# A gated attention stage on one Trainium2 core: the decay's products moved behind the weighted sums, and two ScalarE steps reordered

## What is computed

```python
# q = layernorm(x); k = v = ctx; 4 heads of 64; 64 sequences of 128 tokens
ig = concat(q, k, v) @ igate + b_i;  fg = concat(q, k, v) @ fgate + b_f
cs = cumsum(log_sigmoid(fg))
log_D = where(lower_triangle, cs - cs.T, -inf) + ig.T
m = max(log_D, axis=-1)
D = exp(log_D - m)
C = (qh @ kh.T) / sqrt(64) * D
normalizer = maximum(abs(sum(C, axis=-1)), exp(-m))
h = (C / (normalizer + 1e-6)) @ vh
x = x + tanh(g) * (layernorm_per_head(h) * outnorm_scale)
```

## Time and profile before

| | us |
|---|---|
| three runs | 1446.23, 1447.42, 1459.62 |
| median | 1447.42 |
| span of the profiled execution, first to last instruction | 1446.3 |

### The profile page before, as it was taken

The page is one execution under the profiler, slowest core; times in us unless marked ns, Lnnn a source line. Parts: engine busy times, 40 slices in busy tenths (PEclk is TensorE's granted clock), DMA queues, the critical chain, the costliest instruction groups (busy, mean ns, idle before and its releaser), DMA issues.

```text
span 1446.3 us, 30872 instructions
## 1 busy us (share of the span) xinstructions
PE 1327.5 (92%) x11617; PEld 896.8 (62%) x11672; DVE 1163.6 (80%) x1888; ACT 1050.8 (73%) x1739; POOL 769.1 (53%) x1225
## 2 busy tenths in 40 slices
PE   4799999999999999999997999999889988579898
PEld 3466666666666666666654666666667666434376
DVE  3577887887888878877786999998656899979988
ACT  2377777777777777777764988888745665689897
POOL 2156666767668667675767333441302586878100
PEclk9999999999999999999987999999999998889999
DMA  9666867758668576676530000000255463229099
GB/s 151 112 127 110 132 114 132 133 97 150 107 122 136 99 144 112 108 124 105 90 98 1 1 1 1 1 1 1 70 157 149 105 163 96 51 122 401 1 379 377
DMA packets 124964, 165.71 MB, mean 115 GB/s; under 512 B 47362, under 2 KB 78210, under 8 KB 120450
## 3 DMA queue, kind: packets, MB, share of 16 engines
q1 hardware_dynamic: 124048, 162.95, 49.8%
q10 hardware_dynamic: 768, 0.79, 0.5%
HBM read 76.07 MB, written 35.65 MB: 77 GB/s over the span
## 4 chain that ended last, share of the span: by engine, by line
PE 64%; DVE 13%; ACT 11%; issue 4%; POOL 4%; DMA 2%; SPq 1%; ACTq 0%; DVEq 0%; POOLq 0%
PE psum L574 10%; PE psum L585 10%; PE psum L561 7%; PE psum L602 5%; PE psum L549 4%; PE psum L619 4%; PE psum L982 4%; PE psum L1013 3%; ACT f_gelu L2071 3%; PE psum L1005 3%; ACT f_gelu L2063 2%; PE psum L523 2%; PE psum L536 2%; POOL a_fac L1772 2%; PE psum L612 2%
## 5 line engine op out<-in xcount | busy, mean ns | idle before, releaser
L764 DVE TENSOR_REDUCE neg_max<-psum 128x8 f32<-128x1024 f32 x256 | 313.1, 1223 | 67.9 <-PE psum L561 63.2
L695 ACT ACTIVATE exp_t<-psum 128x512 f32<-128x512 f32 x512 | 281.5, 597 | 49.6 <-PE psum L574 49.5
L869 POOL TENSOR_TENSOR rs<-rs,minus_half 128x16 f32<-128x16 f32 x64 | 186.4, 2912 | 5.0
L574 PEld LDWEIGHTS psum<-q_stack,k_stack 50*128 50x128 f32 x2048 | 135.0, 188 | 77.5 <-issue 73.2
L574 PE MATMUL psum<-q_stack,k_stack 50*128 50x128 f32 x2048 | 171.1, 287 | 0.8 <-ACT exp_t L695 0.8
L585 PE MATMUL psum<-exp_t,v_pad 128*32 128x256 f32 x2048 | 165.8, 396 | 0.0
L561 PE MATMUL psum<-k_stack,q_stack 48*128 48x256 f32 x1024 | 133.4, 339 | 14.9 <-DVE neg_max L764 11.3
L700 ACT ACTIVATE o_t<-psum 128x512 f32<-128x512 f32 x128 | 76.7, 599 | 89.9 <-PE psum L585 89.8
L861 POOL TENSOR_TENSOR sq<-u 128x256 f32<-128x256 f32 x64 | 39.3, 614 | 171.6 <-DVE u L781 170.6
L982 PE MATMUL psum<-f_w,f_xqt 128*128 128x512 bf16 x481 | 117.0, 383 | 6.9 <-DVE f_hid L1118 3.7
L561 PEld LDWEIGHTS psum<-k_stack,q_stack 48*128 48x128 f32 x1024 | 80.6, 188 | 66.9 <-issue 48.5
(11 more groups left out here) (232 smaller groups left out, 3078.8 us busy)
## 6 DMA issues: line engine op xcount, KB each, us to landing
k_stack<-k_hi SPq DMA_DIRECT2D x252, 128.0 KB, 4.7
g_scratch<-f_gelu SPq DMA_DIRECT2D x18, 1024.0 KB, 4.7
k_stack<-k_lo SPq DMA_DIRECT2D x126, 128.0 KB, 5.0
f_gelu<-g_scratch SPq DMA_DIRECT2D x12, 1024.0 KB, 11.5
ctx_t<-in_ctx_t SPq DMA_DIRECT2D x32, 256.0 KB, 5.3
x_state<-in_x SPq DMA_DIRECT2D x16, 512.0 KB, 7.0
v_in<-in_ctx SPq DMA_DIRECT2D x32, 256.0 KB, 5.6
v_scratch<-v_in SPq DMA_DIRECT2D x32, 256.0 KB, 5.4
```

Source lines behind the costliest of these rows:

```text
L574: r = e.matmul(psum[:, 2 + j, o:o + P], self.k_st[rows, b // 2 % self.NK, pair // 2 % 2, pair % 2, i, pair // 4, b % 2, :], self.q_st[rows ...
L695: e.activation(self.prob[:, n % 3, j].rearrange("p n w t -> p (n w t)"), psum[:, 2 + j, :], ACT.Exp).then_inc(s["exp"], 1)
L764: e.tensor_reduce(self.negm[:, b % 2, :, :, 2 * u:2 * u + 2].rearrange("p j w n -> p j n w"), psum[:, 0:2, :].rearrange("p j (n w k) -> p ...
L869: e.tensor_tensor(self.rs[:, i], self.rs[:, i], self.expo[:, :], ALU.pow).then_inc(s["pool"], 1)
```

## The change

TensorE: `arg(i + 1)` moves from behind `scores(i)` and `gates` to the end of the pass, behind `weighted(i - 1)`, `place`, `turn` and `columns(1)`; the next thing after it is `scores(i + 1)`. Inside `arg` both mask products come first and both rows' products after them, where they alternated. ScalarE: `numerator(i - 1)` and `turned` move ahead of `decay_exp(i + 1)`; `square` and `next_normed` stay behind it. No instruction and no wait is added or removed.

```diff
@@ def arg(p):
             for b in range(2):
                 e.matmul(psum[:, 2 + b, :], self.ident16[:, :], self.mask16[:, :, :].rearrange("p n t -> p (n t)"), start=True, stop=False)
+            for b in range(2):
                 r = e.matmul(psum[:, 2 + b, :], self.a_row[0:35, p % 2, :], self.m_row[0:35, p % 2, b].rearrange("r n t -> r (n t)"),
                              start=False, stop=True)
             r.then_inc(s["arg"], 1)
@@ TensorE's loop
             made = self.late_group(i - 2)
             if made is not None:
                 gates(made)
-            if i + 1 < self.NP:
-                arg(i + 1)
             if 0 <= i - 1:
                 weighted(i - 1)
             if made is not None:
                 place(made)
...
             if i == 14:
                 columns(1)
+            if i + 1 < self.NP:
+                arg(i + 1)
             if i == 24:
                 self.fw.pe_rows(w, 7)
@@ ScalarE's loop
             if self.late_group(i - 2) is not None:
                 gates(self.late_group(i - 2))
+            if 0 <= i - 1 < self.NP:
+                numerator(i - 1)
+            for n in range(2):
+                if self.late_group(i - n) is not None:
+                    turned(self.late_group(i - n), n)
             if i + 1 < self.NP:
                 decay_exp(i + 1)
             if 0 <= i - 1 < self.NP:
-                numerator(i - 1)
                 square(i - 1)
...
-            for n in range(2):
-                if self.late_group(i - n) is not None:
-                    turned(self.late_group(i - n), n)
             if i == 11:
                 log_forget(1)
```

## The result

The changed kernel takes 1443.17 us (median of 20 runs, 1440.92 to 1465.15), beside 1448.97 for the kernel before (20 runs, 1446.23 to 1471.36). The ratio is 0.9956, 95% interval 0.9941 to 0.9972: faster by 0.4%, which is inside the 1% that the prediction called "within 1%". The ratio leaves out three slow runs (two of the changed kernel, one of the kernel before), each over 1.5% above the fastest of its kernel. The profiled executions have spans of 1446.3 and 1441.6 us.

What follows compares the result with a forecast made beforehand. TensorE was taken to bound the kernel up to pair 11, VectorE after. Gains of 3.6 + 1.7 + 0.2 = 5.5 us, less GpSimd's 0.55, left 5.0 off 1447.42: 1442.4 us, range 1440.5 to 1447.5.

Steps and rivals of the forecast that it cites:

- Term 1: TensorE, each pass up to pair 11: four fewer changes of row depth save 0.40 us, 3.6 us over nine passes.
- Term 2: TensorE's `gates` no longer wait for ScalarE's `turned`: 0.43 us in each of passes 4, 6, 8, 10, 1.7 us.
- Start: `arg(0)` is 0.2 us shorter by two changes; pass 1 keeps only that, since `scores(2)` waits for its keys.
- Rival C: Loads: keys come late, nine passes each wait 0.2 to 0.6 us, most of the depth gain lost; 1446.0 us, chance 0.08.
- Sum at pair 11: Gain by `combine(11)`: 3.6 + 1.7 + 0.2 = 5.5 us.
- GpSimd: Behind pair 11, `add(6)` waits 0.70 us for `scaled(6)` and the next power starts late: loss 0.55, leaving 5.0 us.
- Moved steps: Moving `weighted`, `decay_exp`, `square`, `numerator` and the rows' loads in the pass costs nothing.
- Rival A: Longer TensorE gaps drop its clock to 0.50; four slow stretches at 2.2 us cost 8.8: 1451.2 us, chance 0.12.
- Rival B: 35 and 64 rows are different modes, or 0.32 is not the depth change: 1445.0 us, chance 0.17.

Runs made afterwards that it cites:

- the rows at full depth: Changed kernel with both operands of the rows' products 128 rows deep instead of 35, the added rows being zeros; 1443.58 us.
- The run with late copies: Changed kernel with ScalarE's copies of the queries (`turned`) back behind `square`; 1447.02 us.
- the kernel with more filling products: Changed kernel with 18 instead of 6 filling products before `scores(14)`; 1443.46 us.
- The cheap factor: Kernel before and changed kernel, each with GpSimd's power replaced by a product, as a test only; 1453.54 and 1433.54 us, not to be compared.
- moving only `scaled(6)`: Changed kernel with `scaled` of pair 6 on VectorE instead of GpSimd, and 18 filling products before `scores(14)`; median 1440.06 us, ratio to before 0.9921.
- ScalarE's order alone: Kernel before with `numerator` and `turned` ahead of `decay_exp`, TensorE as before; 1449.79 us.
- TensorE's alone: Kernel before with the mask and rows' products grouped and `arg` behind `weighted`, ScalarE as before; 1456.5 us.
- the alternating order: Changed kernel with the products of `arg` back in the order mask, rows, mask, rows; 1454.92 us.
- the changed kernel's second profile: Changed kernel run again unaltered, in five rounds; median 1442.68 us, ratio to before 0.9936.

## Why the prediction was right, and where its steps were off

The forecast was 1442.4 us with a range of 1440.5 to 1447.5; 1443.17 was measured. The gain in the stage was 5.84 where 5.0 was forecast. That the time came within 0.8 us is in part luck. The forecast stood on 1447.42, the median of three runs; the median of twenty is 1448.97, 1.55 higher, and the medians lie 5.80 apart instead of 5.0. The base was too low and the gain too small, and the two errors partly cancel. So do two inside the gain: 1.6 too little at pair 11, and 0.6 too little for what GpSimd takes back.

- **Term 1, the changes of row depth.** Right in mechanism and unit: 0.20 to 0.21 for two changes at the old place and at the new one. 35 and 64 rows do run without a change between them. Mis-sized in what it left out: the nine passes gained 0.51 each rather than 0.40. The 0.1 is the pair of `scores` products beside the rows' product, shown by the rows at full depth. The upper bound in the prediction (0.44) was too low, for it counted changes only and had no case in which products overlap.
- **Term 2, the gates' wait.** 0.96 - 0.51 = 0.45 per pass with gates, 0.43 forecast. The run with late copies shows the step to be needed as well: without it the wait is 1.23.
- **Start.** 0.56 at `combine(2)` instead of 0.2. My step was that `scores(2)` keeps waiting for its keys. They landed just in time in this profile. In other runs of the same code they didn't: the timeline of TensorE in the kernel with more filling products has
```profile
1090.57 1.16 PE L1441 MATMUL psum<-a_qt,a_kt 64*128 64x128 f32 x16 [0.40 <-DMA a_kt<-in_ctx_t]
```
  and `combine(2)` at 7.06, `combine(3)` at 11.58 (10.87 after). So 0.7 of the 7.1 is luck of the landing; Rival C happened in pass 2 and in no other.
- **Sum at pair 11.** 7.10 for 5.5: 1.0 from the nine passes (0.11 each, nearly all of it the overlap), 0.4 from the start, and 0.1 from each of term 2 and of passes 8 and 9, where VectorE, the next bound, lets go 1.59 instead of 1.47.
- **GpSimd.** Right that it takes back between pairs 11 and 12, wrong in the way and the size: 1.12 instead of 0.55. I had it as a wait of `add(6)` for `scaled(6)`, and so held only `add(6)` against the end of `scaled(6)` (0.53 in hand). In truth a small VectorE product ahead of `add(6)`, which had 0.22 in hand, now stands beside `scaled(6)` and does not end before it. The kernel before pays this already at later pairs; the change brings pair 6 into it. The cheap factor (gain 6.12 at pairs 11, 12 and 31) shows that the loss is GpSimd's; moving only `scaled(6)` shows which operation.
- **Moved steps.** They cost nothing, as said. But the reason is narrower than I wrote. ScalarE's order alone and TensorE's alone lose 0.9 and 6.9 us in the stage; each creates a wait that the other takes away. I had checked the pair and did not see how near the neighbours were. In the changed kernel `combine` waits last for the exponential and no longer for the scores (0.63 before `combine(11)`), as I had allowed; TensorE shows no gap for it up to there.
- **Rival A, the clock.** Its events came: gaps of 1.74 and 1.54 before `scores` are followed by 0.50. Its price did not: from `combine(12)` to `combine(31)` the changed kernel's two profiles take 104.33 and 103.67 us, the kernel before 104.20, because VectorE stays the bound at half clock (6.30 of 6.80 us busy, and 13.16 of 13.60). The sum that I had called the whole price, 8.8, is near what the alternating order paid (8.6 over pairs 25 to 31, against the changed kernel's second profile), but there it was one stretch of 37 us; that the two sums are alike is chance.
- **Rival B** falls with the 0.01 between a rows' product and `scores`.

The Trainium skill's "TensorEngine Tiling (Array Packing)", Key Properties, has that changing the tiling mode drains TensorE. The trace agrees: 0.105 us for each change between 128 rows and 35 or 64, at the granted clock of 1.00 (2.4 GHz).

## What to carry to other kernels

Put matmuls of like contraction depth next to each other, and shallow ones that lie on different row halves next to each other too: here the first was worth 0.4 us per pass and the second 0.1. When an order changes on one engine, follow the ring through the engine beside it before pricing the parts; here TensorE's part and ScalarE's part each lose time without the other. When a stage gets shorter, look also at the small products of an engine for what they will now stand beside, and not only at the ones that wait. And measure from the stage's first instruction: it came between 1081.59 and 1098.51 us in these profiles, a spread of nearly three times the change's worth.

## What the runs showed of the hardware that I had not expected

- A VectorE product of 16 columns takes 0.99 to 1.29 us instead of 0.17 when it starts 0 to 0.31 us behind a GpSimd product of 512 columns (1.26 to 1.29 us), though neither reads what the other writes. Its end moves to the other's end, to 0.04, in all of the places named above, in both kernels.
- A product of 35 rows and two of 64 rows are worked on side by side: they start 0.01 apart, and behind the rows' products 14 are left, which take 1.05 us where 16 take 1.16.
- TensorE's clock was seen at 0.50 at gaps of 1.54, 1.74, 2.82 and 3.22 us in one profile of the changed kernel; with one gap of 3.22 filled down to 0.63 it stayed full, once. A gap of 2.00 was followed by 0.50 in the changed kernel's second profile, and by 1.00 in the kernel with more filling products: the gap alone does not tell. With the alternating order it stayed at 0.50 for 37 us while TensorE was busy all but 0.5 of 33.4: a busy TensorE is no pledge of a fast one.
